# A graph network on one core: second norm scores four node blocks at once, store lead counted per block, destination column loaded in 98 pieces

## The reference, cut to what matters

```
h = relu(layernorm(x))
# first layer: three spline convolutions over 125 = 5*5*5 kernel cells
out[i] = 1/deg(i) * sum over edges (row=i, col=j) of basis(edge) @ (x[j] @ W[cell]) + b
# conv 1 takes ones (64 outputs), conv 2 takes conv 1's result gathered at col=dst (64 -> 64),
# two small dense layers make a shift of the attributes; conv 3 gathers h (32 -> 32)
x = x + conv3
# second layer: attention and a recurrent gate
h = relu(layernorm(x))
feat = h @ W_gat ; el = feat . attn_l ; er = feat . attn_r    # 4 heads
e = leaky_relu(el[src] + er[dst]) ; softmax over dst ; sum ; GRU ; x + elu(...)
```

## Time and profile before

| | |
|---|---|
| median of 3 runs | 10590.01 us (10586.35 to 10597.7) |
| the profiled execution | 10569.67 us |
| its span, first to last instruction | 10567.9 us |
| PE, PEld busy | 54%, 46% |
| DVE busy | 73% |
| ACT, POOL busy | 28%, 61% |
| mean granted TensorE clock | 0.782 |

### The profile page before, as it was taken

How to read it: one execution, slowest core, us unless ns; L and a number is a source line. 1 busy time by engine, 2 the same in 40 slices (tenths; PEclk the granted TensorE clock), 3 DMA queues, 4 the chain that set the end, 5 groups by cost and what they waited for, 6 DMA issues and landing times. The chain is left out here.

```text
span 10567.9 us, 178994 instructions
## 1 busy us (share of the span) xinstructions
PE 5739.3 (54%) x38968; PEld 4901.6 (46%) x38968; DVE 7680.9 (73%) x17252; ACT 2918.3 (28%) x8407; POOL 6414.5 (61%) x6574
## 2 busy tenths in 40 slices
PE   3366666666377499999999455555555201000010
PEld 2255566555377377777777355555554200000000
DVE  9966666666499477777777476766766188999998
ACT  0022222222133244444444244444443001111111
POOL 6077777777100566666665566666663377777773
PEclk9987777777799799999999788888887555555555
DMA  1040000000933455555555344444444122222221
GB/s 48 3 117 3 3 3 3 3 3 3 20 41 39 90 105 105 104 105 104 103 105 97 52 68 68 68 68 68 68 68 59 20 64 64 62 62 62 67 62 46
DMA packets 2181778, 608.41 MB, mean 58 GB/s; under 512 B 2007975, under 2 KB 2141607, under 8 KB 2181476
## 3 DMA queue, kind: packets, MB, share of 16 engines
q1 hardware_dynamic: 1078132, 311.05, 16.1%
q0 software_dynamic: 218016, 193.97, 10.7%
q10 hardware_dynamic: 885584, 102.89, 7.6%
HBM read 430.75 MB, written 176.23 MB: 57 GB/s over the span
## 5 line engine op out<-in xcount | busy, mean ns | idle before, releaser
L1228 PE MATMUL c_acc<-c_spread_sb,c_basis_sb 128*125 128x256 f32 (+1 forms) x12544 | 2438.9, 361 | 1149.9 <-DVE c_basis_sb L1103 864.2
L1228 PEld LDWEIGHTS c_acc<-c_spread_sb,c_basis_sb 128*125 128x125 f32 x12544 | 2150.0, 219 | 1401.8 <-issue 1018.9
L976 POOL DMA_INDIRECT c_ring<-hid_table,c_at x1568 | 1512.2, 964 | 758.7 <-issue 446.1
L614 POOL DMA_INDIRECT rec<-rk_rec,rk_place x1568 | 1646.6, 1050 | 516.1 <-issue 471.9
L1353 ACT ACTIVATE c_sums<-c_acc 125x512 f32<-125x512 f32 (+1 forms) x3136 | 1460.5, 491 | 1752.2 <-PE c_acc L1228 1270.8
L1651 POOL DMA_INDIRECT at_ring<-gat_table,at_place x1568 | 1483.0, 946 | 758.5 <-issue 753.9
L976 POOL DMA_INDIRECT c_ring<-feat_table,c_at x1568 | 1489.1, 950 | 659.2 <-issue 439.7
L1087 DVE TENSOR_TENSOR c_spread_sb<-c_mesh,c_rin 128x512 f32<-128x512 f32 (+1 forms) x3136 | 1738.6, 554 | 60.2
L1908 PE MATMUL gr_hps<-ident,gr_hs 128*32 128x128 f32 x98 | 29.8, 408 | 1976.0 <-DVE gr_xs L1742 1938.0
L497 DVE CUSTOM_DVE_ANT_0 rk_junk_l<-rk_look_ps,rk_hi 128x98 bf16<-128x98 f32 x1568 | 401.7, 256 | 765.3 <-PE rk_look_ps L559 764.9
L1908 PEld LDWEIGHTS gr_hps<-ident,gr_hs 128*32 128x32 f32 x98 | 6.3, 108 | 1990.3 <-DVE gr_xs L1742 1952.1
(11 more groups left out here) (362 smaller groups left out, 9207.4 us busy)
## 6 DMA issues: line engine op xcount, KB each, us to landing
c_rin<-rows SPq DMA_DIRECT2D x3136, 42.0 KB
c_rin<-rows SPq DMA_DIRECT2D x3136, 20.0 KB
rows<-c_ring ACTq DMA_DIRECT2D x408, 128.0 KB, 2.5
rows<-c_ring ACTq DMA_DIRECT2D x408, 72.0 KB, 2.5
rows<-rk_blank SPq DMA_DIRECT2D x112, 252.0 KB
rows<-at_ring SPq DMA_DIRECT2D x196, 144.0 KB
rec<-rk_rec,rk_place POOLq DMA_INDIRECT x1568
c_ring<-hid_table,c_at POOLq DMA_INDIRECT x1568
```

Source lines behind the costliest of these rows:

```text
L614: pool.indirect_dma_start(out=d.rec, out_offset=bass.IndirectOffsetOnAxis(ap=place[:, u, j:j + 1], axis=0), in_=rec[:, u, j, :], in_offset ...
L976: pool.indirect_dma_start(out=ring[:, u, j, :], out_offset=None, in_=table, in_offset=bass.IndirectOffsetOnAxis(ap=at[:, h, u, j:j + 1], a ...
L1228: last = pe.matmul(acc[pp % BANKS][:, (w % 2) * WN * feats:(w % 2 + 1) * WN * feats], basis[:, q, w, :, :].rearrange("p a b -> p (a b)"), ...
```

## The change

In the first convolution the one DMA on ACT's queue goes. After each block's record load SP now issues a DMA of 2048 words of the same column (128 partitions of 16 words), and SP, not ACT, waits at the end until all have landed. The lead is worked out from `need` of each block, less four slots for each block before it, in place of the pair's end in turns of 4096 edges. The second norm transposes four blocks at once (128x128, 25 groups, seven batches of up to four groups), multiplies by a 128x32 block-diagonal matrix of weights, issues the next batch's transposes ahead of this batch's scores, and copies all scores in two instructions at the end; the weights are made before the norm.

```
 count_and_prefix
-  end = min(end of pair i + 128, EP); end_i = (end + 4095) >> 12
-  lead = max(1, max over pairs of (end_i - i))
+  chain(dve.tensor_copy(need[:, :], c.need[:, 0, :]))
+  chain(dve.scalar_tensor_tensor(need[:, :], c.ramp[0:1, 0:NB], -float(RING // 2), need[:, :], ALU.mult, ALU.add))
+  chain(dve.tensor_reduce(lag4[:, 0:1], need[:, :], X, ALU.max))
+  chain(dve.tensor_scalar(lag4[:, 0:1], lag4[:, 0:1], float(RING - 1), None, ALU.add))
+  chain(dve.tensor_copy(end_i[:, 0:1], lag4[:, 0:1]))
+  chain(dve.tensor_scalar(end_i[:, 0:1], end_i[:, 0:1], RING.bit_length() - 1, None, ALU.logical_shift_right))
...
 conv_of_ones, SP, after the load of block b (share = NT // NB = 16)
+  sp.dma_start(c.dst_at[:, bass.ds(b * share, share)].unsqueeze(2),
+               d.rec[bass.ds(b * (share * P), share * P), 1:2].rearrange("(t p) w -> p t w", p=P)
+               .bitcast(U32)).then_inc(indexed, 16)
 conv_of_ones, ACT
-  act.dma_start(c.dst_at[:, 0:NT].unsqueeze(2), d.rec[0:EP, 1:2].rearrange("(t p) w -> p t w", p=P).bitcast(U32)).then_inc(indexed, 16)
...
-  act.wait_ge(indexed, 16)
...
 second_norm, PE
-  for s in range(NB // SET):
-      if s:
-          pe.wait_ge(copied, s)
-      for j in range(SET):
-          last = pe.transpose(turned_ps[:, j * P:(j + 1) * P], c.h[:, s * SET + j, :], c.ident[:, :])
-      last.then_inc(turned, 1)
-      pe.wait_ge(copied, s + 1)
-      if s:
-          pe.wait_ge(scored_taken, s)
-      for j in range(SET):
-          last = pe.matmul(score_ps[:, 8 * j:8 * j + 8], h_t[:, j * P:(j + 1) * P], score_w[:, :], start=True, stop=True)
-      last.then_inc(scored, 1)
+  turn(0)
+  for s in range(batches):
+      if s + 1 < batches:
+          turn(s + 1)
+      score(s)
 second_norm, DVE
-  for s in range(NB // SET):
-      dve.wait_ge(scored, s + 1)
-      chain(dve.tensor_copy(c.elr[:, s * SET:(s + 1) * SET, :], score_ps[:, 0:8 * SET].rearrange("p (j k) -> p j k", k=8)))
+  dve.wait_ge(scored, batches)
+  chain(dve.tensor_copy(c.elr[:, 0:split, :].rearrange("p b k -> p (b k)"), score_ps[0][:, 0:split * 2 * HEADS]))
+  chain(dve.tensor_copy(c.elr[:, split:NB, :].rearrange("p b k -> p (b k)"), score_ps[1][:, 0:(NB - split) * 2 * HEADS]))
```

More of the change, by code:

```diff
@@ L727, in body @@
                     .then_inc(loaded[r], 16)
+                with nc.allow_non_contiguous_dma(reason="one word of each record"):
+                    sp.dma_start(c.dst_at[:, bass.ds(b * share, share)].unsqueeze(2),
+                                 d.rec[bass.ds(b * (share * P), share * P), 1:2].rearrange("(t p) w -> p t w", p=P)
+                                 .bitcast(U32)).then_inc(indexed, 16)
+            share = NT // NB
             ahead_loop(sp, c.block_passes[:, 0:1], body, begin=next_pass)
+            n = sp.value_load(c.block_passes[:, 0:1], min_val=1, max_val=EP // BROWS + 1)
+            sp.wait_ge(indexed, n * (NB * 16))
+            sp.sem_inc(sp_turn, 1)
         @block.vector
@@ L1461, in second_norm @@
     loaded, chain_sem, cleared = sem("n2_loaded"), sem("n2_chain"), sem("n2_cleared")
-    var_ready, std_ready, weights_ready, normed, turned, copied, scored, scored_taken = (
-        sem(f"n2_{x}") for x in ("var", "std", "weights", "normed", "turned", "copied", "scored", "scored_taken"))
+    var_ready, std_ready, normed, turned, copied, scored = (
+        sem(f"n2_{x}") for x in ("var", "std", "normed", "turned", "copied", "scored"))
     made, stored = sem("n2_made"), sem("n2_stored")
     full = (N // P) * P
-    cols = SET * P
+    fold = P // FEAT
+    groups = -(-NB // fold)
+    batch = 4
+    batches = -(-groups // batch)
+    tail = NB - (groups - 1) * fold
     with nc.Block() as block, ExitStack() as ctx:
@@ L1469, in second_norm, with members, blocks_in @@
         bias = sb("n2_bias", [P, FEAT])
[L1470 to L1473, removed]
+        wg = sb("n2_wg", [P, HEADS * FEAT])
+        attn = sb("n2_attn", [P, 2, HEADS * FEAT])
+        prod = sb("n2_prod", [P, 2, HEADS * FEAT])
+        score_w = sb("n2_score_w", [P, 2 * HEADS])
+        wide_w = sb("n2_wide_w", [P, fold, 2 * HEADS])
         tmp, stat = sb("n2_tmp", [P, NB, FEAT]), sb("n2_stat", [P, 3, NB])
-        h_t = sb("n2_ht", [FEAT, cols])
+        h_t = sb("n2_ht", [P, 2, batch * P])
         table = sb("n2_table", [P, NB, GW])
-        turned_ps, score_ps = ps("n2_tp", [FEAT, 1024]), ps("n2_sp", [P, 512])
+        turned_ps = [ps(f"n2_tp{u}", [P, batch * P]) for u in range(2)]
+        score_ps = [ps(f"n2_sp{u}", [P, 512]) for u in range(2)]
+        width = 2 * HEADS * fold
+        per_bank = 512 // width
+        def members(s):
+            return range(s * batch, min(groups, (s + 1) * batch))
+        def blocks_in(g):
+            return fold if g < groups - 1 else tail
         @block.sync
@@ L1484, in _ @@
             sp.dma_start(c.x[0:N - full, NB - 1, :], d.x[full:N, :]).then_inc(loaded, 16)
[L1485 removed]
+            for k in range(fold):
+                sp.dma_start(wg[k * FEAT:(k + 1) * FEAT, :], d.W_gat).then_inc(loaded, 16)
             for k, a in enumerate((d.attn_l, d.attn_r)):
[L1487 removed]
+                sp.dma_start(attn[:, k, :], bc(a.rearrange("(a h) f -> a (h f)", a=1), [P, HEADS * FEAT]))\
                     .then_inc(loaded, 16)
@@ L1496, in _ @@
             act.activation(stat[:, 2, :], stat[:, 1, :], ACT.Sqrt).then_inc(std_ready, 1)
-            for s in range(NB // SET):
+            for s in range(batches):
+                rows = blocks_in(members(s)[-1]) * FEAT if len(members(s)) == 1 else P
                 act.wait_ge(turned, s + 1)
-                if s:
-                    act.wait_ge(scored, s)
-                act.activation(h_t[:, :], turned_ps[:, 0:cols], ACT.Copy).then_inc(copied, 1)
+                if s > 1:
+                    act.wait_ge(scored, s - 1)
+                act.activation(h_t[0:rows, s % 2, 0:len(members(s)) * P], turned_ps[s % 2][0:rows, 0:len(members(s)) * P],
+                               ACT.Copy).then_inc(copied, 1)
@@ L1503, in _, with turn @@
         @block.tensor
         def _(pe):
-            pe.wait_ge(normed, 1)
-            for s in range(NB // SET):
-                if s:
-                    pe.wait_ge(copied, s)
-                for j in range(SET):
-                    last = pe.transpose(turned_ps[:, j * P:(j + 1) * P], c.h[:, s * SET + j, :], c.ident[:, :])
-                last.then_inc(turned, 1)
-                pe.wait_ge(copied, s + 1)
-                if s:
-                    pe.wait_ge(scored_taken, s)
-                for j in range(SET):
-                    last = pe.matmul(score_ps[:, 8 * j:8 * j + 8], h_t[:, j * P:(j + 1) * P], score_w[:, :],
-                                     start=True, stop=True)
-                last.then_inc(scored, 1)
+            def turn(s):
+                if s > 1:
+                    pe.wait_ge(copied, s - 1)
+                for k, g in enumerate(members(s)):
+                    n = blocks_in(g)
+                    last = pe.transpose(turned_ps[s % 2][0:n * FEAT, k * P:(k + 1) * P],
+                                        c.h[:, g * fold:g * fold + n, :].rearrange("p b f -> p (b f)"), c.ident[:, :])
+                last.then_inc(turned, 1)
@@ new lines, in score @@
+            def score(s):
+                pe.wait_ge(copied, s + 1)
+                for k, g in enumerate(members(s)):
+                    n = blocks_in(g)
+                    at = g % per_bank * width
+                    last = pe.matmul(score_ps[g // per_bank][:, at:at + n * 2 * HEADS],
+                                     h_t[0:n * FEAT, s % 2, k * P:(k + 1) * P],
+                                     wide_w[0:n * FEAT, 0:n, :].rearrange("p b k -> p (b k)"), start=True, stop=True)
+                last.then_inc(scored, 1)
@@ L1520, in _ @@
+            pe.wait_ge(normed, 1)
+            turn(0)
+            for s in range(batches):
+                if s + 1 < batches:
+                    turn(s + 1)
+                score(s)
         @block.vector
@@ L1523, in _ @@
             dve.memset(c.x[:, :, :], 0.0).then_inc(cleared, 1)
-            dve.wait_ge(loaded, 96)
+            chain(dve.memset(wide_w[:, :, :], 0.0))
+            dve.wait_ge(loaded, 16 * (5 + fold))
             chain(dve.tensor_tensor(c.sum3[:, :, :], c.sum3[:, :, :], bc(c.rdeg[:, :].unsqueeze(2), [P, NB, FEAT]),
```

26 lines of the change are left out of this document (11 added, 15 removed).

## The result

The changed kernel takes 10880.18 us in the median (10864.94 to 10894.61), the kernel before 10591.15 in the same job: a ratio of 1.0273 [1.0256, 1.0289], slower by 289 us where +317 was forecast. The profiled execution took 10864.94 us, 295.3 us more than that of before.

What follows compares the result with a forecast made beforehand. No engine was taken as full throughout; each stage has its own limit (DVE first convolution, PE second, loads third). Terms -79 - 54 - 74 + 304 + 220 = +317 us gave 10907 us, range 10660 to 11090 us.

Steps and rivals of the forecast that it cites:

- The verdict and its cause: Second and third convolutions: slower overall, as odd blocks' loads wait for their own pair's first store; +317 us in all.
- Second convolution, +304 us: Steady pairs of the second convolution: 38 late odd blocks, each 8.0 us longer, because loads wait for a store.
- Third convolution, +220 us: Steady pairs of the third convolution: 38 late odd blocks, each 5.8 us longer; bounds 4 and 8 each.
- nothing absorbs it, since DVE already waits for them: Third convolution: loads beginning 5.8 us later were to lengthen the pair by all of that.
- Starts, -74 us: Start of second and third convolutions: eight fewer slots stored before the first sums, -37 us each; bounds -80 and -30.
- Second norm, -54 us: Second norm: 80.9 us of rounds replaced by batches of about 25 us plus 2 us in front; bounds -49 and -58.
- the work in front: Before the second norm's batches: three more weight loads, a memset, four small copies; 2 us, bounds 1 and 4.
- Part 1, -79 us: First convolution, column in pieces: 87.3 us of store stall go, 8 us return through slower stores; bounds -90 and 0.
- the piece's cost on a store, 0.41 us: First convolution: a third of a piece's 1.25 us of DMA work falls on a store, giving 6.33 us a block.
- the rival that makes them the pace: First convolution: pieces make stores the pace, at most 7.17 us each, so part 1 gains nothing; 10986 us, chance 9%.
- The cited rule on joining transfers: First convolution: skill's advice to join small transfers; at 2.0 us each, 98 pieces on the path would cost 196 us.
- The clock rival: Second convolution: PE, idle before late halves, gets 1.2 GHz; 7.04 us more per late pair, 267 us, 11174 us, chance 7%.

Runs made afterwards that it cites:

- e4: The kernel before with only the lead's rule changed to the new one (one turn): 10963.40 us, ratio 1.0370 to the kernel before.
- e6: The changed kernel with SP waiting for the slots of each half block separately, lead and stores unchanged: 10326.54 us, ratio 0.9774 to the kernel before.
- e1: The changed kernel with the lead computed by the old rule (two turns), nothing else undone: 10420.97 us, ratio 0.9858 to the kernel before.
- e8: The changed kernel itself, unaltered, run again in the later job: 10794.35 us, ratio 1.0218 to the kernel before.
- e7: The changed kernel with each column piece loaded a second time into a spare tile nothing reads: 10792.72 us, ratio 1.0211 to the kernel before.
- e3: The changed kernel with each column piece issued by ACT behind its block's store, not by SP: 10832.33 us, ratio 1.0243 to the kernel before.

## Why the prediction was right, point by point

- **The verdict and its cause**: right. Slot 8i + 8, the first store of the pair itself, is what the odd block's loads wait for. e4 shows the lead as the sole cause of the loss, e6 shows that the one wait makes all of it. The wait closes on 39 pairs, the number counted in the prediction.
- **Second convolution, +304 us**: 308. Each link was right: 3.37 us from store to load (3.55 forecast), 10.77 from load to DVE (10.6), 8.4 us a late pair (8.0).
- **Third convolution, +220 us**: 169, or 4.4 us for each of the 38 late pairs and not 5.8, near the low bound of 4. The failed step is "nothing absorbs it, since DVE already waits for them". The odd half did start late by what was forecast: in the mean of the steady pairs 15.9 us after the pair's first store, where it was 10.0 before. But from there to the next first store it took 32.8 us and not 34.4, so 1.6 us of the 5.9 were absorbed. The slack is shown by e1 and e6: with pairs of 44.4 us their odd half starts 11.2 and 11.5 us after the store. So the loads, for which DVE waited 0.5 us, did not set the pair's pace. Part of the slack lay in DVE's waits for ACT's hats (`c_hat`, values that ACT prepares for the basis). The waits of DVE from 6500 to 7500 us (us in total, times, longest), before:

```profile
DVE c_hat L1147 <- ACT c_hat L673: 201.3, 85, 3.4
DVE c_rel L1113 <- DMA c_trow<-move: 16.7, 33, 0.9
```

in e1, which has the old lead:

```profile
DVE c_hat L1153 <- ACT c_hat L673: 108.6, 89, 2.0
DVE c_rel L1119 <- DMA c_trow<-move: 102.8, 78, 1.9
```

and changed:

```profile
DVE c_rel L1118 <- DMA c_trow<-move: 174.7, 64, 7.5
DVE c_hat L1152 <- ACT c_hat L672: 85.0, 83, 4.4
```

  In e1 nearly half of the wait for hats has gone over to the loads and the pair is no longer. With only the lead different, from e1 to the changed kernel, the loads' wait grows by 72 us and the hats' falls by 24. What moved the one to the other in e1 stays open. The forecast added the delay to the old pair, and the old 34.4 us behind the odd half held slack.
- **Starts, -74 us**: -79 (-45 and -34).
- **Second norm, -54 us**: -56. PE's part is 17 us and not 25, since a batch takes 2.46 us and not 2.8 to 3.7; the work in front (3.5 us more, bounds 1 and 4) and the wait for the attention's start (4.2 us more) took some of it back.
- **Part 1, -79 us**: -45 in the first job, -87 and -99 in the next two. The stall went everywhere. Mis-sized was the piece's cost on a store, 0.41 us. In the first job stores stood at 6.83 us, the side of the rival that makes them the pace, though not its full 7.17, and it cost half of the gain; in the last they stood at 6.15 and cost nothing. There the part passed its bound of -90, since the stall was sized too small as well: a second wait of DVE, 7.09 us for PE, stood behind the 87.32 before, and the first records come 3.9 us earlier without the large load (DVE starts on them 11.2 us after the stage's start in e8 and 15.0 before). The rule on queues that was cited with that rival (Trainium skill, "DMA: Bandwidth & Descriptors", section "Queues, rings and completion order") would have a piece delay a store; the runs agree that it does, and a second piece a block adds 0.25 us to the median store interval (e7). That taking turns between queues is the reason is not shown, since a piece on the store's own queue (e3) left the stores as far apart as one on SP's (e1).
- **The cited rule on joining transfers** (the same page, "Rules for kernel authors"): the change came out against it, since 98 pieces in place of one transfer made the stage 45 to 99 us shorter. But the gain is that the large load no longer stands ahead of the stores; no run put one large transfer on SP's queue, so the rule itself is not tested. The 2.0 us of "Anatomy of one DMA" are given there for DMAs that GpSimd issues. The pieces are issued by SP, land 3.8 us after their issue (median, 3000 to 3200 us, changed kernel) and do so beside the path.
- **The clock rival**: its mechanism is there, its price is not. Four stretches of the changed kernel, PE's gap, the late half, the half after and the mix:

```profile
4496.00:4501.00 5.00, 0.00 (x0) 0.00 (x0) 4.43 (x7) 1.43 (x6) 3.77 (x5) 0.80 0.64 120
4501.00:4510.00 9.00, 8.84 (x30) 7.34 (x31) 7.92 (x13) 3.80 (x7) 6.86 (x8) 0.73 0.48 94
4511.00:4518.00 7.00, 7.00 (x33) 5.83 (x33) 4.50 (x8) 4.42 (x8) 5.48 (x6) 1.00 0.70 128
4519.00:4533.00 14.00, 14.00 (x130) 9.25 (x130) 13.33 (x21) 0.17 (x1) 5.12 (x6) 1.00 0.35 59
```

  After 5.5 us without work PE has 0.73 of its clock in the mean, a mix of its two levels (1.2 and 2.4 GHz), and the half takes 9.46 us (9.22 in the pair above) in place of 7.04. The second half runs at full clock and waits for DVE, so little of that is left. In the pair above DVE waits 0.75 us for PE before its second half; over the late pairs its second half starts 9.4 us behind its first, where it was 9.2 before. The price is some tenths of a microsecond a pair at most, and not 7.04.
- **Luck**: the sum is nearer than its parts. In the first job part 1 came out 34 us worse than forecast and the third convolution 48 us better (135 for 183). In the last job the same change cost 228 us (10794.35 against 10565.86), mostly because the first convolution was 54 us shorter.

## What to carry to other kernels

A prefetch distance is to be counted against the last thing that a consumer needs, in the unit in which it is made: 4b + 5 slots rounded up to one turn of eight looks sufficient and turns a free wait into a loop through the whole pair. When a wait closes such a loop, add up the loop's own links from store to store, and ask of each link taken from the old trace how much of it is waiting that can go: in the second convolution the old links were right within 0.4 us a late pair, in the third they held 1.6 us of slack. Before buying distance with a longer start, split the wait by what each half really needs: here (e6) that kept the short start, and the pairs were as short as with the longer lead.

## What the runs showed of the hardware

- The same stage had its stores 6.83, 6.34 and 6.15 us apart in the median in three jobs (changed kernel, e1, e8), at DMA shares of 0.51, 0.56 and 0.50; with DVE's pace of 6.25 us between them, the same change gained 45 us there in one job and 99 in another.
- PE was granted 0.73 of its clock in the 9 us after a gap of 5.5 us, and 1.00 in the half block after that; single matmuls took 380 ns in the median and up to 782 in the late half.
- One load of 200704 words of 4 bytes held the next DMA of its queue 98.48 us in its issue; as 98 loads on another queue it held none.
- Three register reads on ACT (TENSOR_LOAD, 0.27 us each) and what stands between them filled 1.8 us ahead of one store, in which the sums waited; moved, the wait moved with them.
